# Reciprocals spread over the attention output by DMA, swaps issued by ScalarE, all scores in one run of TensorE

## The reference

```
sim = jnp.einsum('bid,bjd->bij', q, k) * scale
sim = jnp.where(causal[None], sim, -jnp.inf)
attn = jax.nn.softmax(sim, axis=-1)
out = jnp.einsum('bij,bjd->bid', attn, v)
out = out.reshape(b, h, t, d).transpose(0, 2, 1, 3).reshape(b, t, h * d)
return out @ Wo + bo
```

## Time and profile before

| | |
|---|---|
| median of 3 runs | 805.8 us (804.55 to 809.03) |
| the profiled execution: its time, its span | 798.51 us, 796.7 us |
| busy PE, PEld | 755.9 us (95%), 535.0 us (67%) |
| busy DVE, ACT, POOL | 667.4 us (84%), 592.2 us (74%), 572.0 us (72%) |
| TensorE clock granted, mean | 0.997 |
| DMA | 144.66 MB, mean 182 GB/s |

### The profile page before, as it was taken

How to read it: one execution, slowest core, us unless ns; L and a number is a source line. 1 busy time by engine, 2 the same in 40 slices (tenths; PEclk the granted TensorE clock), 3 DMA queues, 4 the chain that set the end, 5 groups by cost and what they waited for, 6 DMA issues and landing times.

```text
span 796.7 us, 20539 instructions
## 1 busy us (share of the span) xinstructions
PE 755.9 (95%) x5763; PEld 535.0 (67%) x5763; DVE 667.4 (84%) x2514; ACT 592.2 (74%) x1678; POOL 572.0 (72%) x701
## 2 busy tenths in 40 slices
PE   8899999999999999999999989999998899999995
PEld 4455666666666566666666656666656579999995
DVE  6688888999899879998999899989987974235997
ACT  3688878878878777877887768777877756565677
POOL 3686767558765877677768886976786266989983
PEclk9999999999999999999999999999999999999998
DMA  4576666456755566556555655565557667434525
GB/s 152 188 224 200 214 203 201 165 191 197 227 180 174 174 200 195 188 180 210 175 186 191 194 173 186 186 199 173 177 179 225 222 193 207 109 85 125 163 90 163
DMA packets 110719, 144.66 MB, mean 182 GB/s; under 512 B 13392, under 2 KB 86352, under 8 KB 110608
## 3 DMA queue, kind: packets, MB, share of 16 engines
q1 hardware_dynamic: 106240, 134.49, 53.8%
q0 software_dynamic: 4224, 8.72, 3.3%
q10 hardware_dynamic: 144, 0.13, 0.1%
HBM read 61.42 MB, written 45.17 MB: 134 GB/s over the span
## 4 chain that ended last, share of the span: by engine, by line
PE 67%; POOL 13%; DVE 8%; issue 7%; DMA 3%; ACT 1%; SPq 0%; DVEq 0%; POOLq 0%; ACTq 0%
PE AO L1109 15%; PE S_all L1068 14%; PE TB L1089 9%; PE AO L1129 5%; PE S_all L1256 4%; POOL yrows L956 4%; PE TB L1269 2%; POOL shared L973 2%; PE AO L1269 2%; DVE Sm L1609 2%; DMA qk<-shared 2%; DVE x_acc L1630 1%; PE TB L1000 1%; POOL shared L722 1%; PE TB L998 1%
## 5 line engine op out<-in xcount | busy, mean ns | idle before, releaser
L1376 ACT ACTIVATE Pr_all<-Sm,nmax 128x512 f32<-128x512 f32 (+3 forms) x512 | 281.8, 563 | 23.7 <-DVE nmax L1609 22.9
L1609 DVE CUSTOM_DVE_ANT_0 Sm<-S_all,causal 128x512 f32<-128x512 f32 (+3 forms) x512 | 223.0, 482 | 46.0 <-PE S_all L1068 45.9
L1068 PE MATMUL S_all<-qk 64*128 64x512 f32 (+3 forms) x1024 | 169.8, 446 | 10.9 <-DVE nmax L1609 8.6
L717 POOL TENSOR_TENSOR qk<-shared,qk 128x512 f32<-128x512 f32 x64 | 81.9, 1280 | 129.6 <-DMA qk<-shared 119.9
L1109 PE MATMUL AO<-PT,shared 128*64 128x128 f32 x1008 | 149.6, 438 | 13.1 <-issue 12.7
L1386 ACT ACTIVATE PT<-TB 128x768 f32<-128x768 f32 x189 | 107.8, 605 | 61.2 <-PE TB L1089 61.2
L1630 DVE SCALAR_TENSOR_TENSOR x_acc<-AO,rinv,x_acc 128x128 f32<-128x128 f32 x504 | 141.7, 344 | 3.5 <-POOL x_acc L769 1.3
L1068 PEld LDWEIGHTS S_all<-qk 64*128 64x128 f32 x1024 | 79.7, 187 | 82.6 <-issue 56.9
L1089 PE MATMUL TB<-ident,Pr_all 128*128 128x128 f32 x764 | 109.2, 279 | 3.6 <-ACT PT L1386 3.1
L1089 PEld LDWEIGHTS TB<-ident,Pr_all 128*128 128x128 f32 x764 | 82.0, 141 | 44.4 <-issue 40.6
L1109 PEld LDWEIGHTS AO<-PT,shared 128*64 128x64 f32 x1008 | 66.5, 136 | 61.1 <-issue 30.9
(11 more groups left out here) (335 smaller groups left out, 1459.0 us busy)
## 6 DMA issues: line engine op xcount, KB each, us to landing
turns<-turned_pr SPq DMA_DIRECT2D x63, 512.0 KB
PT<-turns SPq DMA_DIRECT2D x252, 128.0 KB
qk<-shared SPq DMA_DIRECT2D x124, 256.0 KB
wo<-in_wo SPq DMA_DIRECT2D x64, 64.0 KB, 3.1
PT<-yrows SPq DMA_DIRECT2D x7, 512.0 KB, 4.3
w_tile<-in_wup SPq DMA_DIRECT2D x10, 256.0 KB, 3.5
xt<-xrows SPq DMA_DIRECT2D x32, 65.0 KB, 2.7
x_acc<-in_x SPq DMA_DIRECT2D x8, 256.0 KB, 3.4
```

The costliest lines, as they stand in the source:

```text
L717: nc.gpsimd.tensor_tensor(qT[p][:, :], q_cos, qT[p][:, :], ALU.add).then_inc(q_ready, 1)
L1068: nc.tensor.matmul(SB[2 * (group % 2) + h][:, at:at + (qb + 1) * P], qT[p][half, qb * P:qb * P + P], kT[p][half, 0:(qb + 1) * P], start=Tr ...
L1376: nc.scalar.activation(Pr[j][:, 0:n], Sm[j], ACT.Exp, bias=nmax[:, j:j + 1], scale=-1.0, accum_out=rsum[p][:, h * QB + qb:h * QB + qb + 1] ...
L1609: nc.vector.tensor_tensor_reduce(out=Sm[j], in0=SB[2 * (group % 2) + h][:, at:at + n], in1=causal[:, T - n:T], scale=-0.125, scalar=HUGE, ...
```

## The change

- Scores: groups 0, 1 and 2 run one after the other, each in banks of its own (0 in SB[0:2], 1 in SB[2:4], 2 in both banks of TB). `project_out` comes after all three.
- Banks: the transpose of group 1 moves to SB[0:2], the v projection to SB[2], and y has OB for itself. The transpose of group 2 and the q projection stay in TB, where the scores of group 2 now lie: both wait for all masks of the unit.
- Division: `norm_o` multiplies the attention output (128 x 512, both heads) by a tile of reciprocals, in place of ACT's copy. That tile is made so: `invert` on DVE; `turn_sums` on PE, a transpose of the 128 x 8 reciprocals into SB[0], after the masks of group 0; `take_norms` on DVE, a copy of the 8 x 128 result to SBUF; on SP one DMA of it to DRAM and, once it is stored, two that read it back, each broadcast over 64 partitions (`spread_norms`). DVE waits for it in `norm_o` a unit later.
- `project_out` contracts over both heads at once (4 matmuls) and adds up the 8 pairs of a batch in OB; `add_y` adds OB to x_acc once a batch, in place of `scale_y`, which stays for the last unit alone.
- The swap DMAs are issued by ACT, in the unit after the one in which SP issued them, between the last exponentials of the unit before and the first of this one. SP loads the PT rows straight after it stored them. wo is kept in SBUF after the first batch.
- DVE's order in a unit: norm_o, reciprocals, masks of group 0, take_norms, masks of group 1, turn, masks of group 2, rope_q, routing.

The core of the diff:

```diff
         def turn_banks(u, group):
-            two = TB if u < UNITS - 1 or group == 0 else S_all[:, 2 * group - 2:2 * group, :]
+            two = S_all[:, 0:2, :] if group == 1 else S_all[:, 2:4, :] if group == 2 and u == UNITS - 1 else TB
...
+        def score_bank(group, h):
+            return TB[:, h, :] if group == 2 else SB[2 * group + h]
...
             def project_q(u, n, batch):
                 inputs_ready(n, batch)
-                if u == 2:
-                    pe.wait_ge(v_ready, 2)
-                elif u > 2:
-                    pe.wait_ge(pt_ready, 2 * (u - 3) + 1)
+                if u >= 2:
+                    pe.wait_ge(maxed, BLK * (u - 1))
...
             def transpose(u, p, group):
...
                 elif group == 2:
 
-                    pe.wait_ge(pt_ready, 2 * u + 1)
+                    pe.wait_ge(maxed, BLK * (u + 2))
                 else:
-                    wait(pe, pt_ready, 2 * u)
-                    pe.wait_ge(q_read, min(u + 3, UNITS))
-                    if u == 0:
-                        pe.wait_ge(k_read, 2)
+                    pe.wait_ge(inverted, 2 * u + 2)
...
+            def turn_sums(u, p):
+
+                pe.wait_ge(inverted, 2 * u + 1)
+                pe.wait_ge(maxed, BLK * (u + 1) + DONE_BY[0])
+                nc.tensor.transpose(sums_bank, rinv, ident[:, :]).then_inc(sums_turned, 1)
...
+                for i in range(QB):
+                    last = nc.tensor.matmul(y_bank[:, i * P:i * P + P], OT[p][:, i * P:i * P + P], wo_of(u),
+                                            start=(first and i == 0), stop=last_pair, skip_group_check=True)
...
+            def take_norms(u):
+
+                dve.wait_ge(sums_turned, u + 1)
+                wait(dve, norms_stored, 16 * u)
+                nc.vector.tensor_copy(norms_t, sums_bank).then_inc(inverted, 1)
+
+            def norm_o(u, p):
+
+                dve.wait_ge(pv_done, u + 1)
+                dve.wait_ge(norms_in, 32 * (u + 1))
+                wait(dve, y_done, u - 1)
+                nc.vector.tensor_tensor(OT[p][:, :], o_bank(u), spread_of(u), ALU.mult).then_inc(o_ready, 1)
+
+            def add_y(b):
+
+                dve.wait_ge(y_done, min(PAIRS * (b + 1), UNITS - 1))
+                dve.wait_ge(x_set, b + 1)
+                rows = x_acc[:, b * QB:b * QB + QB, :].rearrange("p a c -> p (a c)")
+                nc.vector.tensor_tensor(rows, y_bank, rows, ALU.add).then_inc(y_read, 1)
...
+            def spread_norms(u, p):
+
+                sp.wait_ge(inverted, 2 * u + 2)
+                wait(sp, norms_in, 32 * (u - 1))
+                sp.dma_start(norms[p * BLK:p * BLK + BLK, :], norms_t).then_inc(norms_stored, 16)
+                sp.wait_ge(norms_stored, 16 * (u + 1))
+                wait(sp, o_ready, u - 1)
...
+                for h in range(2):
+                    sp.dma_start(spread_of(u)[D * h:D * h + D, :],
+                                 norms[p * BLK + QB * h:p * BLK + QB * h + QB, :].rearrange("(o q) t -> o (q t)", o=1).to_broadcast([D, T])).then_inc(norms_in, 16)
```

More of the change, by code:

```diff
@@ L1362, in copy_v @@
                     wait(act, pv_done, VS * (group - 1))
[L1363 removed]
+                nc.scalar.activation(V[group % 2][:, i, :], bank, ACT.Copy).then_inc(v_ready, 1)
             def exp(u, p, j):
@@ L1845, in attention @@
                     dve.wait_ge(pool_set, POOL_SET)
+                if u >= 2:
+                    norm_o(u - 2, p)
+                if not first:
+                    invert(u - 1, 1 - p)
                 mask_max(u, 0)
@@ L1851, in attention @@
                     rope_q(2)
-                if u >= 2:
-                    scale_y(u - 2)
+                if not first:
+                    take_norms(u - 1)
                 for j in range(FIRST_OF[1], FIRST_OF[2]):
                     mask_max(u, j)
-                if not first and not last:
+                if not last:
                     for h in range(2):
@@ L1860, in attention @@
                     mask_max(u, j)
-                if first:
-                    for h in range(2):
-                        turn(u, h)
+                if batch > 0 and n == STATS_AT:
+                    add_y(batch - 1)
                 if not first and u + 2 < UNITS:
@@ L1905, in _ @@
             attention_units(attention)
+            norm_o(UNITS - 2, 0)
             copy_last()
-            scale_y(UNITS - 2)
+            add_y(B - 1)
             def route_last(b):
```

189 lines of the change are left out of this document (115 added, 74 removed).

## The result

The changed kernel takes 879.9 us (median of 4 runs, 878.9 to 883.5) against 806.6 us for the kernel before on the same chip: ratio 1.0916, 95% interval 1.087 to 1.096. It is **73 us slower**. The prediction said 840 us, 820 to 870: the sign was right, the size was less than half of it. The profiled execution has a span of 878.9 us and a time of 880.65 us, 82 us over the span before.

A forecast was written before the change was run, and what follows sets the result against it. PE's program was taken as the bound, lengthened by a PE-DVE loop: 59 x 9.9 = 584, plus 11, 16 and 3 make 614 us against 578, 36 more; less 2 at the start, +34 on 805.8 gives 840 us, range 820 to 870.

The forecast's parts named there:

- The loop: PE and DVE: scores, masks, sums, masks, transpose, q, attend; PE stalls 0.7 us, making the unit 9.9 us.
- The trip: Sums from masks through turn_sums to take_norms, PE and DVE: 0.65 us, bounds 0.2 and 1.0 us.
- what comes on top: Added to the units: routing on PE 11 us, routing on DVE 16 us, POOL's later swaps 3 us.
- this case: The loop as worked out: 822 to 858 us by the bounds of the sums' trip, chance 0.72.
- The start and the end: Outside units 3 to 61: first swap about 2 us sooner from ACT, end unchanged.
- So it fits, narrowly: Reciprocals' store, two issues and load take 5.4 to 7.0 us, up to 7.8, against 7.1 us before norm_o.
- that rival: Reciprocals late for norm_o: each 0.5 us over adds 30 us, 870 us; counted with POOL or ACT, chance 0.15.
- The estimate of 4.6 us from the Trainium skill: Reciprocals' store and loads: 2 + 2.6 us, which would leave the late-reciprocals rival dead.
- The swaps: Swap DMAs issued by ACT: nothing added for ACT, 3 us for POOL.
- Their rival: POOL or ACT holds the loop, ACT waiting for POOL's products; counted with late reciprocals, 850 to 880 us, 0.15.
- The faster rival: VectorE is the pacer, the loop does not bind, PE's own work does: 20 us less, 786 us; chance 0.05.
- no change: Trip at its lower bound and half of DVE's routing hidden: units take 580 us, within 4 us; chance 0.03.

The follow-up runs named there:

- e2: Changed kernel with the reciprocals stored and spread through DRAM in only 4 of 63 units, trip through TensorE and VectorE kept: 846.5 us.
- e10: Changed kernel; ScalarE issues broadcast loads after its group 2 copy, SyncE loads turned blocks next unit, x load behind turned store: 929.3 us.
- e16: Changed kernel with SyncE's queue reordered and ScalarE issuing the broadcast loads ahead of its copy of k: 870.3 us.
- e9: Kernel before, with only the swaps moved from SyncE to ScalarE, at their place in the changed kernel: 834.0 us.
- e15: Changed kernel with the swaps issued by SyncE again, between the store of the turned blocks and its landing: 867.6 us.
- e3: Changed kernel with the third group's masks ahead of turn and the reciprocals stored and spread in 4 units only: 822.8 us.
- e4: Changed kernel with the reciprocals' DMAs, turn_sums and take_norms left out in all but 4 units: 814.6 us.
- e17: Changed kernel with SyncE reordered (turned loads first, swaps back on it), next x load behind the turned loads: 873.8 us.

## Why the prediction was wrong

**The loop: right.** Forecast was the last mask 6.4 us into the unit and 3.5 us behind it, 9.9 us. In unit 17 the last mask is done at 6.4 to 6.5 us, the transposition starts at 6.61, a hand-over of 0.1 to 0.2 us that the sum lacked, and 3.55 us follow: 10.16. The trip was put at 0.65 us and took 0.74. PE's idle a unit was put at 0.7 us and is 0.75 (0.19 ahead of turn_sums, 0.56 ahead of the transposition). The 59 units were put at 614 us; without the reciprocals' DMAs they take 618.5 (e2). Two errors met there: 59 x 10.16 is 599, 15 us over the 584, and what comes on top was 19 us and not 30; that they nearly cancel is luck. The upper end of this case, 858, does not follow from its terms either: two thirds of 20 us are 13, so 853. The project_out of 4 matmuls over 128 channels took 1.05 us where 1.06 was assumed.

**The start and the end: small, with the wrong sign.** Forecast was -2 us for both; it is +3.9 and +7.9. In the first 46.67 us the granted clock was 0.93 in the mean, before 1.00 in the first 42.75, and PE was busy 39.4 for 35.9 us. e2 has the same start (46.28 us), so that part is not the reciprocals' DMAs; why was not tested, nor what makes the end longer.

**The step that failed: "So it fits, narrowly".** The trip of the reciprocals was summed as if SyncE were free: a store, two issues, a load, 5.4 to 7.0 us (7.8 at worst) against 7.1. As the length of a trip that was not far off: 6.8 us by the rows above, 5.0 to 9.8 where norm_o waited. What was not summed is the queue that carries it. In the same unit SyncE stores the turned blocks, stands until they have landed and issues four loads, and it stands for the reciprocals' landing as well. With terms from the earlier trace rows that could have been added up ahead: 2.2 to 3.0 us for the first landing, 1.1 of issues, 2.7 to 4.3 for the second, some 2 for four issues, 8 to 10 us in a unit of 9.9, with no room for the batch's other DMAs; it measured 9.7 in the median. The text said itself that half a microsecond over makes 30 us on top of the loop, 870 in all, and gave that case 0.15. The runs show the loop and the late reciprocals together: 40.4 us and 30.0 in the units (e2), and with the ends, +11.8 where -2 was forecast, the 82 us of the span. By the deciding point of that rival, 7.1 us, a trip of 6.8 in a unit in which SyncE comes 0.5 us late is already over; e10 and e16 show the price of some 2 us, 59 us.

The estimate of 4.6 us from the Trainium skill (DMA: Bandwidth & Descriptors, Anatomy of one DMA) would have called this rival dead. That section describes DMAs that GpSimd issues; these are issued by SyncE. The runs have 1.2 to 4.9 us from the store's issue to the loads' in the changed kernel, 2.6 in the median (the page's 2 us lie inside), and 3.6 to 5.7 us from the loads' issue to their use: the page's sum lacks the two issues of 0.5 us and whatever the broadcast and the other traffic add.

**The swaps: costed at 3 us, and too little.** For ACT the text has "ACT is not late in unit 34, and gets about the same work; nothing.", for POOL 3 us. On the kernel before they cost 27 us (e9), in the changed kernel 12 (e15), which lie inside the lateness. Their rival named the right engines and that ACT now waits for POOL's products, but its sum asked only whether the rotated q and k come in time.

**The faster rival and no change: out, as said.** But e3 and e4 show how near they lay: without the DMAs and with a shorter loop the kernel is within 1 to 2% of before. The work taken off DVE, 82 us, had little to give: PE's idle time in the units, 21.5 us, was the most it could.

**What stays open:** whether SyncE's wait for the rotary products is why order and swaps on it take from each other (e17), what makes the trip 5.0 us in one unit and 9.8 in another, and the 12 to 16 us of stalls that appear in e3 and e4 once the loop is short.

## What to carry to other kernels

A queue that waits for landings is an engine like the others: add up all that it does in one turn of the loop, waits included, and compare the sum with the loop's length before asking whether one transfer fits. A transfer that fits with half a microsecond to spare did not fit here: its own length varied by more than that, and a late one made the next late through the loop. And when work is taken off an engine that is not on the path, look at what the replacement puts on the path: here 0.74 us of hand-overs and a trip through memory for 82 us of VectorE that TensorE hardly waited for.

## What the hardware showed that was not expected

- The same two DMAs issued by ScalarE instead of SyncE, and so at another point of the unit, made the kernel before 27 us slower (e9), at equal bytes.
- A store of 4 KB (8 x 128) was no quicker than one of 64 KB: 2.6 us in the median from its issue to that of the loads that wait for it (1.2 to 4.9, changed kernel), where the trace before had 2.2 us from issue to landing for 64 KB.
- The store of the turned blocks (512 KB) took 3.7 us in the median until its loads were issued with the two broadcast loads issued just ahead of it, and 2.7 us without them (e2).
- Four matmuls over 128 channels in project_out took as long as eight over 64: 1.05 us and 1.06.
